# Maximum rows of the softmax: transposed alone and placed by transfers, in an attention kernel on one Trainium2 core

## The chip, the cores and the metric

The kernel runs on one core of a Trainium2 chip. The engines of the core work side by side, each in its own program's order, and meet at semaphores: PE (matrix products; its weight loads are listed as PEld), DVE (vector), ACT (activation functions and copies), POOL (general) and SP, which only issues DMA transfers here. SBUF is the memory for operands, PSUM the one that PE writes to, in banks of 128 x 512 f32. The metric is the device time of one execution in microseconds, as the median of several runs.

## The reference

Four layers act on x (4 batches, 256 rows, 160 columns) with a context (4, 512, 96). Cut to what matters:

```
def attn(x, ctx, wq, wk, wv, wo, bo, heads):       # 20 heads of 8, or 8 heads of 20
    q, k, v = heads_of(x @ wq), heads_of(ctx @ wk), heads_of(ctx @ wv)
    a = softmax(einsum('bhid,bhjd->bhij', q, k) * dh ** -0.5)
    return heads_joined(einsum('bhij,bhjd->bhid', a, v)) @ wo + bo

x = attn(x, ctx, ...) + x                          # layer 0: cross (u = 0)
for layer in (1, 3):
    x = attn(ln(x), ln(x), ...) + x                # self  (u = 1, 5)
    x = attn(ln(x), ctx, ...) + x                  # cross (u = 2, 6)
    x = (a * gelu(g)) @ ff_w2 + ff_b2 + x          # a, g = split(ln(x) @ ff_w1 + ff_b1)
    # between them layer 2: attention over 508 context rows (enc, u = 3), plus a second
    # one whose queries come from the last 4 context rows and whose keys are x (ca, u = 4)
```

The result is x after layer 3. Everything is f32 outside; softmax subtracts each row's maximum.

## The kernel before

An attention is cut into quads of four heads; there are 116 of them: 60 in cross attention, 40 in self attention, 8 in enc and 8 in ca. Queries and keys are transposed and stacked so that a head takes 32 partitions (20-head attentions, four heads in a group of 128) or 64 (8-head ones, two heads in a group). A head's partitions hold a high and a low part of each value, and two rows for its maximum: in the query stack (`qs20`, `qs8`) two columns for each head, at 3 dh and 3 dh + 1, hold the negated row maximum, as a high and a low part, and the keys hold ones there. The product of the transposed queries `qT` and the keys then already is score minus maximum, and ACT applies the exponential straight to it.

The steps of a quad are:

- `kdma`: SP copies the quad's four key heads from `kdense` to one of four places in `ring` (four transfers)
- `max` (L794 on PE, L1221 on DVE): scores in natural layout into one of two PSUM banks, and their maximum over the keys. Eight units in a cross quad, four in a self quad; `qT` still has zeros in its maximum rows here
- `negm` (L1234, L1235 on DVE): the negated maximum, and its rest, into the query stack
- `mtr` (L808 on PE, L1244 on DVE): the quad's part of the query stack is transposed again, now with the maxima, and copied over `qT`
- `st` (L775 on PE, L1062 on ACT), the slots: transposed scores of two heads and 128 keys, and the exponential. Eight in a cross quad, four in a self quad
- `pv` (L831 on PE) and `oev` (L1069 on ACT): outputs, four heads and 128 keys at a time, and their copy

Before a quad's first attention of a batch, `m_zero` (L1384, POOL) sets the stack's maximum columns to zero, so that the first transposition of the queries (`q_tr`, L938) leaves zeros.

The order of all this is one list, made by `plan()` before the program is written. Each step has a due place among the slots (`put`), a cost and a list of what it needs; `simulate` takes, again and again, the step that can start first on a modelled PE clock. Projections, layer norms, feed-forward and the transposition of queries and keys are background steps, spread among the quads of the other batch of a pair. Each engine then walks through the same list and runs its part of each step. `M_LEAD = 8` puts a quad's `mtr` eight slots before its first one. A step of kind SPARE, `mtr` among them, takes one of three PSUM banks (`sp_ps`) in turn; `taken` is the wait until the bank's reader is done with that step.

## Time and profile before

| | |
|---|---|
| median of 3 runs | 1082.69 us (1079.75 to 1086.96) |
| the profiled execution | 1083.78 us, its span 1082.0 us |
| PE / DVE / ACT / POOL busy | 96% / 64% / 62% / 7% |
| granted PE clock, mean | 0.981 |

The span is the time from the first instruction to the last; what lies around it makes the 1.8 us to the execution's time. A busy engine is not one at its peak: matmuls overlap, and each is shown with its whole latency. Idle time before an instruction is listed with what ended it. A clock of 1.00 stands for 2.4 GHz, one of 0.50 for 1.2 GHz.

### The profile page before, as it was taken

The numbers are of one execution on the slowest core, as the hardware profiler recorded it, in microseconds if no ns is written. First come the engines' busy times: TensorE is split into PE (matmuls) and PEld (weight loads), VectorE is DVE, ScalarE is ACT, GpSimd is POOL, SyncE is SP. The second block draws the span as 40 slices with busy tenths as digits, with TensorE's granted clock in tenths as the row PEclk, the third lists the DMA queues.
The fourth block names the chain that finished last, engine by engine and source line by source line (L and its number), as shares of the span: only waits on it lengthen the run. The fifth ranks groups of instructions, "written<-read, shape, count | busy, mean of one in ns | idle before, by whom it ended". The sixth has DMA issues, their size and how long they took to land.

```text
span 1082.0 us, 21250 instructions
## 1 busy us (share of the span) xinstructions
PE 1034.7 (96%) x7808; PEld 719.5 (67%) x7808; DVE 689.4 (64%) x1603; ACT 675.4 (62%) x1400; POOL 74.0 (7%) x129
## 2 busy tenths in 40 slices
PE   8999989999998999999998998999999899999978
PEld 5656666667685666767685666676768566765646
DVE  3777757875546567875755775787555556777631
ACT  4556666766664666766765665776665556766641
POOL 3000000000002100001010000000100110000000
PEclk9899999999999999999999999999999999999995
DMA  8110001110232101010113010101021400111000
GB/s 195 42 39 17 21 22 44 30 31 11 49 77 56 25 21 45 21 31 22 35 31 89 21 26 20 45 21 31 10 60 30 103 20 22 34 25 40 11 7 7
DMA packets 31150, 40.26 MB, mean 37 GB/s; under 512 B 10324, under 2 KB 22232, under 8 KB 30728
## 3 DMA queue, kind: packets, MB, share of 16 engines
q1 hardware_dynamic: 31048, 38.89, 14.9%
q8 instruction: 65, 1.06, 0.4%
q14 instruction: 37, 0.30, 0.1%
HBM read 10.97 MB, written 0.66 MB: 11 GB/s over the span
## 4 chain that ended last, share of the span: by engine, by line
PE 87%; DVE 5%; ACT 4%; issue 3%; DMA 0%; POOLq 0%; POOL 0%; DVEq 0%; ACTq 0%
PE st_ps L775 18%; PE pv_ps L831 17%; PE mx_ps L794 17%; PE sp_ps L757 8%; PE sp_ps L758 7%; PE sp_ps L876 4%; PE sp_ps L858 3%; DVE mx L1221 2%; PE sp_ps L808 2%; PE sp_ps L950 2%; PE sp_ps L938 2%; PE sp_ps L989 2%; ACT probs L1062 2%; ACT oT L1069 1%; PE sp_ps L893 1%
## 5 line engine op out<-in xcount | busy, mean ns | idle before, releaser
L1221 DVE TENSOR_REDUCE mx<-mx_ps 128x1 f32<-128x512 f32 (+2 forms) x720 | 475.4, 685 | 184.4 <-PE mx_ps L794 181.1
L1062 ACT ACTIVATE probs<-st_ps 128x512 f32<-128x512 f32 x720 | 400.6, 597 | 184.3 <-PE st_ps L775 178.4
L794 PE MATMUL mx_ps<-ring,qT 128*128 128x512 f32 (+2 forms) x864 | 294.9, 400 | 6.9 <-issue 3.8
L775 PE MATMUL st_ps<-qT,ring 128*128 128x256 f32 (+1 forms) x1408 | 276.1, 298 | 5.4 <-ACT probs L1062 3.2
L775 PEld LDWEIGHTS st_ps<-qT,ring 128*128 128x128 f32 (+1 forms) x1408 | 217.8, 190 | 80.4 <-ACT probs L1062 40.6
L831 PE MATMUL pv_ps<-probs,v 128*9 128x256 f32 (+3 forms) x2944 | 223.8, 377 | 3.0 <-ACT probs L1062 2.3
L794 PEld LDWEIGHTS mx_ps<-ring,qT 128*128 128x128 f32 x864 | 143.5, 190 | 88.9 <-DVE mx L1221 45.7
L831 PEld LDWEIGHTS pv_ps<-probs,v 128*9 128x9 f32 (+2 forms) x2944 | 44.9, 90 | 64.3 <-issue 19.2
L1111 ACT ACTIVATE kdense<-sp_ps 128x512 f32<-128x512 f32 (+2 forms) x116 | 57.4, 539 | 24.4 <-PE sp_ps L876 23.9
L1049 ACT ACTIVATE ks<-sp_ps 128x320 fp32r<-128x320 f32 x80 | 35.2, 440 | 42.3 <-PE sp_ps L858 27.5
L876 PE MATMUL sp_ps<-identr,ks 128*128 128x128 f32 (+1 forms) x416 | 59.7, 279 | 0.7 <-DVE qs L1187 0.6
L1351 POOL TENSOR_SCALAR rstd<-mv 128x2 f32<-128x2 f32 x24 | 5.6, 234 | 788.8 <-DVE mv L1258 788.8
L876 PEld LDWEIGHTS sp_ps<-identr,ks 128*128 128x128 f32 (+1 forms) x416 | 55.4, 195 | 3.5 <-DVE ks L1187 0.9
L1069 ACT ACTIVATE oT<-pv_ps 128x256 f32<-128x256 f32 x108 | 41.6, 385 | 24.8 <-PE pv_ps L831 24.2
L1244 DVE CAST qT<-sp_ps 128x256 fp32r<-128x256 f32 (+1 forms) x108 | 47.0, 435 | 14.3 <-PE sp_ps L808 13.2
L757 PE MATMUL sp_ps<-hT,wb 80*128 80x256 f32 x160 | 53.2, 417 | 1.4 <-ACT hT L1121 1.2
L758 PE MATMUL sp_ps<-hT,wb 80*128 80x256 f32 x160 | 52.3, 411 | 0.0
L1304 DVE SCALAR_TENSOR_TENSOR gate<-sp_ps,cols,gate 128x256 f32<-128x256 f32 x40 | 16.8, 478 | 54.1 <-ACT gate L1167 33.6
L808 PEld LDWEIGHTS sp_ps<-identr,qs 128*128 128x128 f32 (+1 forms) x248 | 38.7, 189 | 16.1 <-issue 13.6
L808 PE MATMUL sp_ps<-identr,qs 128*128 128x128 f32 (+1 forms) x248 | 48.3, 282 | 0.3 <-DVE ks L1187 0.3
L1187 DVE TENSOR_TENSOR ks<-sp_ps,ks 128x160 fp32r<-128x160 f32 x80 | 25.1, 317 | 36.4 <-ACT v L1090 21.5
L1293 DVE TENSOR_TENSOR x<-sp_ps,xb 128x320 f32<-128x320 f32 x32 | 15.7, 492 | 39.0 <-PE sp_ps L989 20.8
(134 smaller groups left out, 1050.2 us busy)
## 6 DMA issues: line engine op xcount, KB each, us to landing
ring<-kdense SPq DMA_DIRECT2D x256, 64.0 KB, 2.0
wb<-in_w_blk SPq DMA_DIRECT2D x4, 1400.0 KB, 9.1
ring<-kdense SPq DMA_DIRECT2D x160, 32.0 KB, 1.8
ring<-kdense SPq DMA_DIRECT2D x32, 127.0 KB, 2.3
wd<-in_w_down SPq DMA_DIRECT2D x4, 400.0 KB, 9.5
ring<-oT SPq DMA_DIRECT2D x16, 64.0 KB, 3.2
ctx_n<-in_ctx SPq DMA_DIRECT2D x4, 192.0 KB, 6.6
x<-in_x SPq DMA_DIRECT2D x4, 160.0 KB, 3.3
```

The lines of the kernel that those rows point to most:

```text
L757: pe.matmul(out, lhs[:, 0, :], rhs[:, 0, :], start=True, stop=False)
L758: return pe.matmul(out, lhs[:, 1, :], rhs[:, 1, :], start=False, stop=True)
L775: mm = pe.matmul(st_ps[s % N_ST][0:kr, i * a["nq"]:(i + 1) * a["nq"]], key_op(n, h)[:, c * P:c * P + kr], query_op(u, b)[:, h // of(u), :] ...
L794: mm = pe.matmul(mx_ps[o % N_MX][0:rows, j * a["nk"]:(j + 1) * a["nk"]], query_op(u, b)[:, h // of(u), tt * P:tt * P + rows], key_op(n, h) ...
L808: mm = pe.matmul(bank[:, k * a["nq"] + i * P:k * a["nq"] + i * P + rows], query_stack(u, b)[0:rows, t, g * of(u):(g + 1) * of(u), :].rearr ...
L831: mm = pe.matmul(pv_ps[32 * j:32 * j + a["dh"] + 1, 0:a["nq"]], v, probs[0:kr, s % N_P, i * a["nq"]:(i + 1) * a["nq"]], start=(c == 0), st ...
L876: mm = pe.matmul(bank[:, k * SQ + t * P:k * SQ + t * P + kr], ks[0:kr, t, g * of(u):(g + 1) * of(u), :].rearrange("p h s -> p (h s)"), ide ...
L1062: nc.scalar.activation(probs[0:kr, s % N_P, 0:w], st_ps[s % N_ST][0:kr, 0:w], ACT.Exp, scale=float(a["dh"]) ** -0.5).then_inc(S["probs_rea ...
L1069: nc.scalar.activation(dst, pv_ps[:, 0:ATT[u]["nq"]], ACT.Copy).then_inc(S["out_taken"], 1)
L1111: nc.scalar.activation(dst, bank[:, 0:n * SQ].rearrange("p (g k) -> p g k", g=n)[:, :, 0:w], ACT.Copy).then_inc(free, 1)
L1221: nc.vector.tensor_reduce(mx[b][0:rows, t, heads[0]:heads[-1] + 1], mx_ps[(o - 1) % N_MX][0:rows, 0:a["hpm"] * a["nk"]].rearrange("p (h k) ...
L1244: nc.vector.tensor_copy(query_op(u, b)[:, g0:g1, :].rearrange("p g q -> p (g q)"), bank[:, 0:(g1 - g0) * nq]).then_inc(done, 1)
```

## The change

The second transposition of the query stack goes. The negated maxima of a quad (8 values for each of two tiles of 128 queries) are written to a small tile of their own, `mn`; one matmul transposes it (72 columns wide, so that both tiles' rows come out, at partitions 0 and 64), DVE copies the result to `mT`, and SP puts its rows into the maximum rows of `qT` by transfers of two rows of 128 queries, a high and a low one: eight for a quad of 32-row heads (four heads, two tiles), four in enc, two in ca. That is the new step `mdma`. The first slot of a quad waits for those transfers (`m_in`) and no longer for DVE's copy. `mn` and `mT` exist twice, and DVE waits with the copy for the transfers of two quads before. As the stack's maximum columns are never written now, `m_zero` goes. The planner gives `mtr` a lower cost and `mdma` 400 ns and the latency of a transfer, 2000 ns.

```diff
-        put(hi + MTR_DUE, 3, ("mtr", n))
+        put(hi, 3, ("mtr", n))
+        put(hi, 4, ("mdma", n))
...
+    if kind == "mdma":
+        return 0, [("dma", 400)]
...
-        return TR * groups * len(q_tiles(u)), dve(groups * nq)
+        return TR, dve(P)
...
-            return [("mtr", slots[s]["n"])] + ...
+            return [("mdma", slots[s]["n"])] + ...
...
-        done[step] = t + (DMA_LATENCY if step[0] == "kdma" else HANDOFF)
+        done[step] = t + (DMA_LATENCY if step[0] in ("kdma", "mdma") else HANDOFF)
...
+        mn = [sb(f"mn{i}", [P, TQ, 64], FR) for i in range(2)]
+        mT = [sb(f"mT{i}", [72, P], FR) for i in range(2)]
...
+                    elif step[0] == "mdma":
+                        n = step[1]
+                        u, b, qd = quads[n]["u"], quads[n]["b"], quads[n]["qd"]
+                        k, sr, dh = of(u), ATT[u]["sr"], ATT[u]["dh"]
+
+                        taken(sp, ("mtr", n))
+                        for i, (t, rows) in enumerate(q_tiles(u)):
+                            for j in range(k):
+                                src = mT[n % 2][64 * i + j:64 * i + 8:k, 0:rows].bitcast(F32)
+                                at = slice(sr * j + 3 * dh, sr * j + 3 * dh + 2)
+                                g0, g1 = 4 * qd // k, 4 * (qd + 1) // k
+                                sp.dma_start(query_op(u, b)[at, g0:g1, i * P:i * P + rows].bitcast(F32), src).then_inc(m_in[n % 2], 16)
...
                         if s == quads[n]["start"]:
-                            taken(pe, ("mtr", n))
+                            pe.wait_ge(m_in[n % 2], m_landed[n])
...
-                        for k, g in enumerate(gs):
-                            for i, (t, rows) in enumerate(q_tiles(u)):
-                                mm = pe.matmul(bank[:, k * a["nq"] + i * P:k * a["nq"] + i * P + rows],
-                                               query_stack(u, b)[0:rows, t, g * of(u):(g + 1) * of(u), :].rearrange("p h s -> p (h s)"),
-                                               identr[0:rows, 0:rows], start=True, stop=True)
-                        mm.then_inc(full, 1)
+                        rows = q_tiles(u)[0][1]
+                        pe.matmul(bank[0:72, 0:rows], mn[n % 2][0:rows, :, :].rearrange("p t m -> p (t m)")[:, 0:72],
+                                  identr[0:rows, 0:rows], start=True, stop=True).then_inc(full, 1)
...
-                        link(nc.vector.tensor_scalar(st[:, :, :, 3 * dh], m, -1.0, None, ALU.mult))
...
+                        link(nc.vector.tensor_scalar(out[:, :, 0:4], m, -1.0, None, ALU.mult))
...
-                        nc.vector.tensor_copy(query_op(u, b)[:, g0:g1, :].rearrange("p g q -> p (g q)"),
-                                              bank[:, 0:(g1 - g0) * nq]).then_inc(done, 1)
+                        if n >= 2:
+                            dve.wait_ge(m_in[n % 2], m_landed[n - 2])
+                        rows = q_tiles(u)[0][1]
+                        nc.vector.tensor_copy(mT[n % 2][0:72, 0:rows], bank[0:72, 0:rows]).then_inc(done, 1)
...
-                        nc.gpsimd.memset(query_stack(u, b)[:, tiles[0][0]:tiles[-1][0] + 1, :, 3 * dh:3 * dh + 2].bitcast(F32), 0.0).then_inc(S["m_zeroed"], 1)
```

The plan's new costs move steps. Lines have moved too: in the changed kernel the slots are L800, the maxima L819, the outputs L852, the transposition of the maxima L831. Here is PE's program at the second quad's transposition, in the first cross attention, before:

```order
L794 MATMUL mx_ps0<-ring,qT0 128x512 [waits max_taken,ring_in1,spare_taken2]
L794 MATMUL mx_ps1<-ring,qT0 128x512 [waits max_taken]
L808 MATMUL sp_ps2<-identr,qs200 128x128 [waits negm_ready,spare_taken2]
L808 MATMUL sp_ps2<-identr,qs200 128x128
L794 MATMUL mx_ps0<-ring,qT0 128x512 [waits max_taken]
L794 MATMUL mx_ps1<-ring,qT0 128x512 [waits max_taken]
L775 MATMUL st_ps0<-qT0,ring 128x256 [waits spare_taken2]
L775 MATMUL st_ps0<-qT0,ring 128x256
L775 MATMUL st_ps1<-qT0,ring 128x256 x2
```

and now:

```order
L819 MATMUL mx_ps0<-ring,qT0 128x512 [waits max_taken,ring_in1,spare_taken2]
L819 MATMUL mx_ps1<-ring,qT0 128x512 [waits max_taken]
L831 MATMUL sp_ps2<-identr,mn0 72x128 [waits negm_ready,spare_taken2]
L819 MATMUL mx_ps0<-ring,qT0 128x512 [waits max_taken]
L819 MATMUL mx_ps1<-ring,qT0 128x512 [waits max_taken]
L819 MATMUL mx_ps0<-ring,qT0 128x512 [waits max_taken]
L819 MATMUL mx_ps1<-ring,qT0 128x512 [waits max_taken]
L819 MATMUL mx_ps0<-ring,qT0 128x512 [waits max_taken]
L819 MATMUL mx_ps1<-ring,qT0 128x512 [waits max_taken]
L800 MATMUL st_ps0<-qT0,ring 128x256 [waits max_rows_in0]
```

All six maximum units that the next quad has left stand between the transposition and the first scores now, where there were two; the scores wait for the transfers (`max_rows_in0`) and not for DVE's copy (`spare_taken2`). In the first self attention (quad 12), PE's program from the transposition to the quad's first scores is now:

```order
L831 MATMUL sp_ps0<-identr,mn0 72x128 [waits negm_ready,spare_taken0]
L800 MATMUL st_ps0<-qT0,ring 128x256 [waits probs_ready]
L800 MATMUL st_ps0<-qT0,ring 128x256
L800 MATMUL st_ps1<-qT0,ring 128x256 [waits probs_ready]
L800 MATMUL st_ps1<-qT0,ring 128x256
L852 MATMUL pv_ps<-probs,v200 9x256 [waits probs_ready,out_taken]
L852 MATMUL pv_ps<-probs,v200 9x256 x3
L819 MATMUL mx_ps0<-ring,qT0 128x256 [waits max_taken,ring_in1,spare_taken2]
L819 MATMUL mx_ps0<-ring,qT0 128x256
...
L800 MATMUL st_ps0<-qT0,ring 128x256 [waits probs_ready,max_rows_in0]
```

Two slots, two output groups, three maximum units and one transposition of the background stand between. On SP, the queue of all transfers, a cross quad was one group of four and is now two groups:

```order
L740 DMA ring<-kdense 32x512 [waits scores_full,spare_taken0]
L740 DMA ring<-kdense 32x512 x3
L753 DMA qT<-mT 2x128 [waits spare_taken0]
L753 DMA qT<-mT 2x128 x7
L740 DMA ring<-kdense 32x512 [waits scores_full,spare_taken0]
L740 DMA ring<-kdense 32x512 x3
L753 DMA qT<-mT 2x128 [waits spare_taken1]
L753 DMA qT<-mT 2x128 x7
```

The eight small transfers of a quad stand behind the four ring transfers of the next one, and these behind the small ones of the quad before.

## Rows read from the trace of the kernel before

**Rows 1.** Page parts 1, 2 and 4: engines; the clock by slices; the chain.
```profile
PE 1034.7 (96%) x7808; PEld 719.5 (67%) x7808; DVE 689.4 (64%) x1603; ACT 675.4 (62%) x1400; POOL 74.0 (7%) x129
...
PEclk9899999999999999999999999999999999999995
...
PE 87%; DVE 5%; ACT 4%; issue 3%; DMA 0%; POOLq 0%; POOL 0%; DVEq 0%; ACTq 0%
```

**Rows 2.** Page part 5: line, engine, tiles, count | busy us, mean ns | idle before.
```profile
L794 PE MATMUL mx_ps<-ring,qT 128*128 128x512 f32 (+2 forms) x864 | 294.9, 400 | 6.9 <-issue 3.8
L775 PE MATMUL st_ps<-qT,ring 128*128 128x256 f32 (+1 forms) x1408 | 276.1, 298 | 5.4 <-ACT probs L1062 3.2
L831 PE MATMUL pv_ps<-probs,v 128*9 128x256 f32 (+3 forms) x2944 | 223.8, 377 | 3.0 <-ACT probs L1062 2.3
L808 PE MATMUL sp_ps<-identr,qs 128*128 128x128 f32 (+1 forms) x248 | 48.3, 282 | 0.3 <-DVE ks L1187 0.3
```

**Rows 3.** Timelines of PE, PEld and DVE: start, length, line, tiles, count.
```profile
405.23 1.34 PE L876 MATMUL sp_ps<-identr,ks 128*128 128x128 f32 x10
...
46.45 0.44 PE L808 MATMUL sp_ps<-identr,qs 128*128 128x128 f32 x2
46.82 0.62 PE L831 MATMUL pv_ps<-probs,v 128*9 128x256 f32 x8
47.37 0.74 PE L794 MATMUL mx_ps<-ring,qT 128*128 128x512 f32 x2
...
53.86 0.44 PE L808 MATMUL sp_ps<-identr,qs 128*128 128x128 f32 x2
54.39 0.42 DVE L1244 CAST qT<-sp_ps 128x256 fp32r<-128x256 f32 x1
55.12 0.19 PEld L775 LDWEIGHTS st_ps<-qT,ring 128*128 128x128 f32 x1
```

**Rows 4.** DVE's groups by form; then a handoff in the timeline.
```profile
L1244 DVE CAST qT<-sp_ps 128x256 fp32r<-128x256 f32 x100 | 41.5, 415 | 7.9 <-PE sp_ps L808 7.0
L1244 DVE CAST qT<-sp_ps 128x512 fp32r<-128x512 f32 x8 | 5.5, 692 | 6.4 <-PE sp_ps L808 6.2
L1235 DVE SCALAR_TENSOR_TENSOR qs<-mx,qs 128x8 fp32r<-128x8 f32 x108 | 18.9, 175 | 3.7
...
403.20 0.41 DVE L1244 CAST qT<-sp_ps 128x256 fp32r<-128x256 f32 x1
403.66 0.54 PEld L775 LDWEIGHTS st_ps<-qT,ring 128*128 128x128 f32 x4 [0.61 <-DVE qT L1244]
```

**Rows 5.** SP's queue: L727's durations (min/median/max), then timelines.
```profile
L727 SPq DMA_DIRECT2D ring<-kdense x448: 461/591/2031, 23.8 to 1007.6; - x150
L727 SPq DMA_DIRECT2D ring<-oT x16: 467/597/602, 264.2 to 842.3; - x16
...
52.99 2.41 SPq L727 DMA_DIRECT2D ring<-kdense  x4
13.46 0.70 SPq L703 DMA_DIRECT2D ca_n<-in_ctx  x2
```

**Rows 6.** Page part 6: transfers, count, KB each, median us to landing.
```profile
ring<-kdense SPq DMA_DIRECT2D x256, 64.0 KB, 2.0
wb<-in_w_blk SPq DMA_DIRECT2D x4, 1400.0 KB, 9.1
ring<-kdense SPq DMA_DIRECT2D x160, 32.0 KB, 1.8
```

**Rows 7.** Stretches: us, busy and count by engine, PEclk; and a timeline.
```profile
12.00:23.80 11.80, 9.54 (x62) 7.69 (x61) 1.79 (x5) 9.09 (x24) 1.53 (x4) 1.00 0.94 229
23.80:34.10 10.30, 10.30 (x33) 8.38 (x33) 2.49 (x6) 5.13 (x14) 0.00 (x0) 0.50 0.52 119
40.00:77.00 37.00, 36.49 (x289) 21.16 (x289) 29.50 (x57) 23.25 (x44) 0.00 (x0) 1.00 0.13 31
...
27.57 2.48 PE L876 MATMUL sp_ps<-identr,ks 128*128 128x128 f32 x10
```

More of the change, by code:

```diff
@@ L350, in needs @@
         if kind == "negm":
-            return [("max", step[1], len(quads[step[1]]["items"]) - 1)]
+            return [("max", step[1], len(quads[step[1]]["items"]) - 1)] + ([("mtr", step[1] - 2)] if step[1] >= 2 else [])
         if kind == "mtr":
-            return [("negm", step[1])]
+            return [("negm", step[1])] + ([("mdma", step[1] - 2)] if step[1] >= 2 else [])
+        if kind == "mdma":
+            return [("mtr", step[1])]
         if kind == "st":
             s = step[1]
-            return [("mtr", slots[s]["n"])] + ([("st", s - N_ST)] if s >= N_ST else []) + ([pv_of[s - N_P]] if s >= N_P else [])
+            return [("mdma", slots[s]["n"])] + ([("st", s - N_ST)] if s >= N_ST else []) + ([pv_of[s - N_P]] if s >= N_P else [])
         if kind == "pv":
@@ L574, in build @@
         spare_taken = [sem(f"spare_taken{i}") for i in range(N_SP)]
+        m_in = [sem(f"max_rows_in{i}") for i in range(2)]
         ring_in = [sem(f"ring_in{i}") for i in range(RING)]
@@ L602, in build @@
         ring_dmas = {n: 4 * (n // RING + 1) for n in range(len(quads))}
+        m_landed, n_dma = {}, [0, 0]
+        for q in quads:
+            n_dma[q["n"] % 2] += of(q["u"]) * len(q_tiles(q["u"]))
+            m_landed[q["n"]] = 16 * n_dma[q["n"] % 2]
         used_after, count = {}, 0
@@ L1373, in _ @@
                                                 bias[:, c:c + D].unsqueeze(1).broadcast_to([P, TQ, D]), ALU.add).then_inc(S["x_biased"], 1)
-                    elif kind == "m_zero":
-                        _, u, b = step
-                        first = [q["n"] for q in quads if q["u"] == u and q["b"] == b][0]
-                        before = [q["n"] for q in quads[:first] if q["b"] % 2 == b % 2 and
-                                  (q["u"] == u if u in (3, 4) else ATT[q["u"]]["sr"] == 32)]
-                        if before:
-                            taken(pool, ("mtr", before[-1]))
-                        tiles = q_tiles(u)
-                        dh = ATT[u]["dh"]
-                        nc.gpsimd.memset(query_stack(u, b)[:, tiles[0][0]:tiles[-1][0] + 1, :, 3 * dh:3 * dh + 2].bitcast(F32), 0.0).then_inc(S["m_zeroed"], 1)
 def kernel(**inputs):
```

37 lines of the change are left out of this document (15 added, 22 removed).

## The prediction

> **What bounds the kernel now.** First the page's busy shares and its chain [rows 1]: PE is busy for 96% of the span and carries 87% of the chain, its clock is at 8 or more tenths in every slice but the last. So a saved microsecond of PE can be a saved microsecond of span, and one in which PE waits is a lost one. Then the groups [rows 2]: the scores (L775), the maxima (L794) and the outputs (L831) lead; the transposition that is changed (L808) is 248 matmuls. Their mean durations are latencies that overlap. What a matmul costs is the distance between starts [rows 3]: ten transposing matmuls in 1.34 us make (1.34 - 0.28)/9 = 0.118; a scores slot (two matmuls) or a maximum unit takes about 0.24, a group of eight output matmuls 0.55 (46.82 to 47.37). So priced the program is 845 us of PE: 720 slots 173, 720 maximum units 173, 368 output groups 195, some 1,430 transposes 164, projections and feed-forward 140. The span is 1,082, so the units of PE's program pass at 1.28 us of span for each us of price; the rest is waiting for ACT, for DVE and for signals, mostly in pieces of half a microsecond.
>
> Last, the step itself in that timeline [rows 3]. L808 starts at 53.86, L1244's copy runs 54.39 to 54.81, and 0.31 later PE loads the weights of the next block's scores (55.12), with two maximum units before it. A block of four heads (I call it a quad) lasts 7.41 us here (46.45 to 53.86), and its maximum rows are in place 0.95 us after the transposition starts. That path is short, and it is the one that the change lengthens.
>
> **What is removed.** 248 matmuls become 116, one for each quad: 132 x 0.118 = 15.6 us of PE. I take 13 as gained, as some of it lies where PE will wait anyway. DVE's copy is of 128 columns in place of 256 or 512: 415 ns and 692 ns [rows 4] give 1.08 ns a column and a constant of 138, so an estimated 277 ns; 116 copies save 17 us of DVE, which is not the bound. The DVE operations of a quad's negated maxima (175 ns for the second [rows 4]) stay as they are. The 28 memsets of POOL run beside all else, as POOL is busy 7%: nothing; if they held up a transposition at all, it could only be a gain.
>
> **What is added.** Eight transfers for each quad of 32-row heads (100 quads), four in the enc attention and two in the ca attention (8 each): 848, all issued by SP, after the copy and one after the other. SP does not issue for free [rows 5]: a ring transfer holds its queue for 591 ns (median of 448), and four of them take 2.41 us from first start to last end, so the distance is (2.41 - 0.59)/3 = 0.61. The least rows with few descriptors are two loads of four rows each, 0.70 us together, 0.35 each. These read DRAM and stand at the start; the ring rows go from SBUF to SBUF in mid-kernel, as the new ones do, but with 32 rows. Ends: 0.35 and 0.61. I take 0.55, nearer the ring rows because those of 64 rows (from oT, 597) cost the same as those of 32 (from kdense, 591), so it isn't the number of rows that makes them dear. Landing: 1.8 us for 32 KB and 2.0 for 64 KB [rows 6]; the size matters little, so 1.8 for 1 KB.
>
> The Trainium skill, "DMA: Bandwidth & Descriptors", section on the anatomy of one DMA, puts the fixed cost at about 2.0 us, nearly all of it completion, whatever the size. By that the estimate below would be 0.2 us longer for each quad that waits, some 17 us in all, 1,210 in place of 1,193; the ring rows here agree to within that.
>
> The new path from the matmul to the scores of its quad is then: matmul 0.28 and 0.09 until the copy (54.30 to 54.39), copy 0.28, signal to SP 0.05, seven distances of 0.55, landing 1.80, signal to PE 0.05: 2.55 + 7 x 0.55 = **6.4 us**, where it was 0.95. The 0.05 is from a copy that PE waits for, 403.61 to 403.66 [rows 4]. With 0.35 the path is 5.0, with 0.61 it is 6.8. For four transfers it is 4.2, for two 3.1.
>
> **What hides it.** PE is in order, so only what the program has put between the two counts. The planner allows a transfer step 0.4 us of issue and 2.0 of latency, about 3.3 from matmul to scores, and moves the work so: in the order of the change six maximum units and two output groups lie there in one cross quad, four slots, four maximum units and three output groups in the next. I counted what stands between the two for all 116 quads, priced it as above and multiplied by 1.28:
> - cross attention, 60 quads: mean 6.2 us, but 39 of them are under 6.4, with a mean of 4.9: 39 x 1.5 = 58 us of new waiting
> - self attention, 40 quads: 38 are under 6.4, with a mean of 3.8: 38 x 2.57 = 98 us. Its quads have four slots and not eight, so there is less to put in between
> - enc attention, 8 quads: 6 under 4.2, mean 3.3: 5 us. ca attention: none
>
> Sum 161 us. Part is given back: while PE waits, ACT and DVE empty their buffers, so what follows, up to the next transposition, meets fewer waits. That is 223 us of priced PE work behind the quads that wait; passing at 1.1 in place of 1.28, my guess between 1.28 and the 1.0 of a PE that never waits, it gives back 40.
>
> What is queued behind: SP runs 12 issues a quad now, 4 x 0.61 + 8 x 0.55 = 6.8 us. That is under the 10.3 us that a quad would take on average (1,193/116), so the queue isn't the bound; self attention has the shorter quads, and there the waiting counted above stretches them beyond it. SP's old wait before each group, for the scores of four quads before, is older than all it now stands behind. Four times the block's weights go out on the same queue and take 9 us to land [rows 6]; a quad's transfers behind them could be late by a few microseconds, 4 x 5 = 20 at most, which the range holds. DVE's new wait for the transfers of two quads before is met long before. PE's wait stands at a quad's first scores, and everything behind it on PE waits along; ACT and DVE follow within two buffers.
>
> **The sum.** 1,083.8 (the profiled execution; its span is 1,082.0 and the median of the three runs 1,082.7, so it stands for them) + 161 - 40 - 13 = 1,192: I say **1,193**.
>
> **The rivals.**
> - *The clock falls as well.* PE's clock was at 0.50, which is 1.2 of 2.4 GHz, from 23.8 to 34.1 us; before that came 11.8 us in which PE was busy for 9.54 (81%) [rows 7]. From 40 to 77 it is busy for 36.49 of 37 and the clock is full. With a wait of 2 us in each quad of 10, PE would be busy for about 80%, like the stretch before the fall. At half clock, matmuls cost double (ten in 2.48 us, not 1.34 [rows 7]), so a stretch of 10.3 us loses up to 5 us, less what hides in the waits; one such stretch in every 60 us, at 3.5 us each, is 20 x 3.5 = 70: 1,263. Against it: the waits are short and spread. The Trainium skill, "TensorE: Matmul & The Clock Gate", section on HAM oscillation, describes this case: a loop in which every wait for a DMA lowers the clock again. By that rule the time would be this rival's.
> - *Small transfers are issued at the cheapest distance seen, 0.35.* The path is 5.0 us; the same count gives 64 of waiting, 31 back, 13 gained: 1,083.8 + 20 = 1,104. For it: nothing in the trace shows an SBUF transfer of two rows. Against it: the two sizes of ring transfers cost the same.
> - *The path is hidden and PE's saving remains.* Faster: 1,083.8 - 15.6 = 1,068. It decides where the path is under the planner's own 3.3 us, which is what the order is laid out for, i.e. (3.3 - 2.55)/7 = 0.11 us an issue. The least issue in the rows is 0.35 [rows 5].
>
> **Numbers.** Forecast 0.52; clock 0.22; cheap issues 0.19; hidden 0.04; 0.03 between the last two, within a per cent. Three rounds of this kernel scatter by 0.7%, so 1% is about what can be told. The range takes in 0.42 an issue with the give-back (94 - 35 - 13, 1,130), 0.61 without it (196 - 13, 1,267) and most of the clock's case, which adds to either: 1,125 to 1,300. It leaves out half of the cheapest issues and the hidden case. Faster 0.04, same 0.03, slower 0.93.
>
> **What would show it.** The distance between the new transfers' issues on SP, and their landing; some 6.4 us from the new matmul to the first scores of its quad in place of 0.95 at the least; PE's waits before L800 (the scores) put down to the transfer into qT, more than half of the total in self attention, though it is a third of the quads; PEclk below 9 in slices where the clock's rival holds. I am wrong in the first place if an issue takes under 0.3 us, in the second if PE's waits for DVE and ACT shrink by more than 40 us.

## The result and the profile after

The changed kernel takes **1471.1 us** (median of 4 runs, 1456.0 to 1485.4) against 1083.8 for the kernel before (4 runs, 1079.8 to 1087.0): ratio 1.353, 95% interval 1.341 to 1.365. The forecast was 1,193 with a range of 1,125 to 1,300. The side was right, the size was not: the loss is 387 us where 110 was forecast. The profiled execution is the longest of the four, 1485.4 us with a span of 1483.6; it ran at a lower clock than the other three and is left out of the ratio. The sums below are made against its own span and the 1082.0 of before.

The page, parts 1, 2 and 4, in the order of [rows 1]: engines with busy time, share and instructions; the granted clock in 40 slices; the chain by engine.

```profile
PE 1221.2 (82%) x7676; PEld 820.5 (55%) x7676; DVE 679.5 (46%) x1603; ACT 690.3 (47%) x1400; POOL 71.2 (5%) x103
...
PEclk9788877789876876897998988889989667779896
...
PE 50%; SPq 25%; DMA 10%; DVE 6%; issue 6%; ACT 2%; POOLq 0%; POOL 0%; DVEq 0%; ACTq 0%
```

PE is 132 instructions shorter and 187 us longer busy. Its idle time, span less busy time, was 47 us and is 262. The chain, 87% PE before, now runs for a third through SP's queue and the transfers. The clock read 9 in 38 of 40 slices before; it reads 9 in 11 now, and 6 to 8 in the other 29.

The groups that answer to [rows 2] and the waits behind them (line, what was waited for: us in total, times, longest):

```profile
L800 PE MATMUL st_ps<-qT,ring 128*128 128x256 f32 (+1 forms) x1408 | 336.0, 348 | 189.5 <-DMA qT<-mT 180.4
...
L819 PE MATMUL mx_ps<-ring,qT 128*128 128x512 f32 (+2 forms) x864 | 333.3, 449 | 31.1 <-issue 23.2
L852 PE MATMUL pv_ps<-probs,v 128*9 128x256 f32 (+3 forms) x2944 | 256.8, 430 | 2.9 <-ACT probs L1080 1.4
```

```profile
PE st_ps L800 <- DMA qT<-mT: 180.4, 87, 9.1
...
PEld mx_ps L819 <- issue: 85.6, 139, 7.6
...
PEld st_ps L800 <- ACT probs L1080: 57.1, 114, 0.8
...
PEld mx_ps L819 <- DVE mx L1239: 48.9, 99, 1.0
```

The first row of the waits is the change: 180 us at the first scores of 87 quads, where the forecast had 161 us in 83. Two more things are to be seen in the groups. The same 1,408 score matmuls have a mean of 348 ns in place of 298, the maxima 449 in place of 400, the outputs 430 in place of 377. And the weight loads' waits for ACT's and DVE's buffers, 57.1 and 48.9, did not shrink; before they were:

```profile
PEld mx_ps L794 <- DVE mx L1221: 45.7, 113, 0.7
...
PEld st_ps L775 <- ACT probs L1062: 40.6, 98, 0.7
```

The step itself, in the timelines of PE, DVE and SP (start, length; the wait before it in brackets):

```profile
57.38 0.22 PE L831 MATMUL sp_ps<-identr,mn 128*72 128x128 f32 x1
...
60.65 1.10 PE L819 MATMUL mx_ps<-ring,qT 128*128 128x512 f32 x2 [0.18 <-DVE mx L1239]
64.28 1.22 PE L800 MATMUL st_ps<-qT,ring 128*128 128x256 f32 x4 [2.53 <-DMA qT<-mT]
...
66.85 0.31 PE L831 MATMUL sp_ps<-identr,mn 128*72 128x128 f32 x1
...
73.88 0.50 PE L800 MATMUL st_ps<-qT,ring 128*128 128x256 f32 x2 [1.63 <-DMA qT<-mT]
```

```profile
58.08 0.28 DVE L1261 CAST mT<-sp_ps 72x128 fp32r<-72x128 f32 x1
```

```profile
58.39 4.86 SPq L753 DMA_DIRECT2D qT<-mT  x8
63.36 2.43 SPq L740 DMA_DIRECT2D ring<-kdense  x4
67.51 5.27 SPq L753 DMA_DIRECT2D qT<-mT  x8
72.90 2.43 SPq L740 DMA_DIRECT2D ring<-kdense  x4
```

```profile
L753 SPq DMA_DIRECT2D qT<-mT x832: 562/563/682, 36.7 to 1438.8; - x167
```

Matmul at 57.38, copy 58.08 to 58.36, eight issues from 58.39 to 63.25, scores at 64.28: a path of 6.90, and 7.03 for the next quad (the median of the 83 quads of 32-row heads that wait is 6.91). An issue holds the queue 0.563 us, and eight in 4.86 us make a distance of (4.86 - 0.563)/7 = 0.614. The last issue starts at 62.69 and its rows are in 1.59 us later. The row on SP also shows how tight its queue is here: small ones, keys, small ones, keys, with the keys of the next quads issued only when the small ones are out.

Last, the clock. Stretches of the same timeline (length; busy time and count on PE, PEld, DVE, ACT, POOL; PEclk; DMA share; GB/s):

```profile
48.80:62.50 13.70, 11.92 (x91) 6.04 (x83) 9.88 (x18) 6.49 (x13) 0.00 (x0) 1.00 0.09 22
62.50:69.30 6.80, 4.76 (x21) 3.31 (x22) 0.63 (x3) 2.58 (x5) 0.00 (x0) 0.50 0.16 39
69.30:86.40 17.10, 12.54 (x94) 6.41 (x93) 11.36 (x21) 6.97 (x14) 0.00 (x0) 1.00 0.07 18
```

At 62.5, inside the wait of 2.53 us, the clock goes to 0.50, 1.2 GHz, and is back at 2.4 GHz at 69.3. In the kernel before, the stretch from 40 to 77 was at full clock without a break [rows 7]. The clock stands at 1.00 or at 0.50, so the mean over the span, 0.832, makes 2 x (1 - 0.832) x 1483.6 = 498 us at half clock; before, 0.981 makes 41. The 498 us lie in 61 stretches. What that costs is what the experiments have to show: it can be the slower matmuls, or something else can lengthen the busy time.

### The profile page after: what moved, and what is told of

The parts are those of the page before. It is cut to its first block, busy times and chain, and to the rows that moved or that the text cites. A ratio compares the mean times of both kernels' runs of the same rounds, so it can differ in the third digit from the quotient of the medians.

```text
span 1483.6 us, 21914 instructions
## 1 busy us (share of the span) xinstructions
PE 1221.2 (82%) x7676; PEld 820.5 (55%) x7676; DVE 679.5 (46%) x1603; ACT 690.3 (47%) x1400; POOL 71.2 (5%) x103
## 4 chain that ended last, share of the span: by engine, by line
PE 50%; SPq 25%; DMA 10%; DVE 6%; issue 6%; ACT 2%; POOLq 0%; POOL 0%; DVEq 0%; ACTq 0%
SPq L753 23%; PE st_ps L800 13%; DMA qT<-mT 9%; PE mx_ps L819 8%; PE pv_ps L852 7%; PE sp_ps L782 6%; PE sp_ps L783 5%; DVE mx L1239 3%; PE sp_ps L897 3%; PE sp_ps L956 2%; PE sp_ps L879 2%; PE sp_ps L1007 1%; DVE mT L1261 1%; SPq L740 1%; PE sp_ps L968 1%
## 5 line engine op out<-in xcount | busy, mean ns | idle before, releaser
L800 PE MATMUL st_ps<-qT,ring 128*128 128x256 f32 (+1 forms) x1408 | 336.0, 348 | 189.5 <-DMA qT<-mT 180.4
L800 PEld LDWEIGHTS st_ps<-qT,ring 128*128 128x128 f32 (+1 forms) x1408 | 260.1, 228 | 295.5 <-DMA qT<-mT 209.8
L819 PE MATMUL mx_ps<-ring,qT 128*128 128x512 f32 (+2 forms) x864 | 333.3, 449 | 31.1 <-issue 23.2
L852 PE MATMUL pv_ps<-probs,v 128*9 128x256 f32 (+3 forms) x2944 | 256.8, 430 | 2.9 <-ACT probs L1080 1.4
L819 PEld LDWEIGHTS mx_ps<-ring,qT 128*128 128x128 f32 x864 | 167.8, 223 | 136.6 <-issue 82.3
L1261 DVE CAST mT<-sp_ps 72x128 fp32r<-72x128 f32 (+1 forms) x116 | 32.3, 279 | 141.4 <-PE sp_ps L831 141.4
L852 PEld LDWEIGHTS pv_ps<-probs,v 128*9 128x9 f32 (+2 forms) x2944 | 47.0, 92 | 80.0 <-issue 39.8
L897 PE MATMUL sp_ps<-identr,ks 128*128 128x128 f32 (+1 forms) x416 | 70.0, 307 | 1.8 <-DVE ks L1205 1.0
L897 PEld LDWEIGHTS sp_ps<-identr,ks 128*128 128x128 f32 (+1 forms) x416 | 65.7, 224 | 8.2 <-issue 5.2
L968 PE MATMUL sp_ps<-ident,oT 128*128 128x128 f32 x216 | 34.5, 297 | 14.1 <-ACT oT L1087 13.8
L782 PE MATMUL sp_ps<-wb,hT 80*128 80x160 f32 (+1 forms) x128 | 44.1, 431 | 1.2 <-ACT hT L1147 0.8
```

The lines of the kernel that those rows point to most:

```text
L782: pe.matmul(out, lhs[:, 0, :], rhs[:, 0, :], start=True, stop=False)
L800: mm = pe.matmul(st_ps[s % N_ST][0:kr, i * a["nq"]:(i + 1) * a["nq"]], key_op(n, h)[:, c * P:c * P + kr], query_op(u, b)[:, h // of(u), :] ...
L819: mm = pe.matmul(mx_ps[o % N_MX][0:rows, j * a["nk"]:(j + 1) * a["nk"]], query_op(u, b)[:, h // of(u), tt * P:tt * P + rows], key_op(n, h) ...
L852: mm = pe.matmul(pv_ps[32 * j:32 * j + a["dh"] + 1, 0:a["nq"]], v, probs[0:kr, s % N_P, i * a["nq"]:(i + 1) * a["nq"]], start=(c == 0), st ...
L897: mm = pe.matmul(bank[:, k * SQ + t * P:k * SQ + t * P + kr], ks[0:kr, t, g * of(u):(g + 1) * of(u), :].rearrange("p h s -> p (h s)"), ide ...
L968: mm = pe.transpose(bank[0:rows, k * P:(k + 1) * P], src, ident[:, :])
```

## The experiments

The theory after the result: the loss is idle time of PE (215 us more) and, caused by it, half clock (457 us more), which makes the busy time 187 us longer. The rivals: the new order of the steps is what costs; SP's queue holds the keys back, whoever waits; the transfers disturb by their number; the planner's wrong prices are the cause.

**A. The new order with the old data flow** (`e5_order`): the kernel before, its planner changed as in the diff, its transposition and copy untouched.

```diff
+        put(hi, 4, ("mdma", n))
-        return TR * groups * len(q_tiles(u)), dve(groups * nq)
+        return TR, dve(P)
-        done[step] = t + (DMA_LATENCY if step[0] == "kdma" else HANDOFF)
+        done[step] = t + (DMA_LATENCY if step[0] in ("kdma", "mdma") else HANDOFF)
```

> The kernel before, data flow and all (second transposition of the query stack, no small transfers), with its steps in the order that the changed planner makes, but for some ties. With no transfer on any path this is the price of the new order alone. Theory O2 (the order, which keeps the scores back 3.3 us behind the transposition, costs what is left in the kernel with two transfers, 1,181 us): 1,150 to 1,185. If what is left there is the two transfers' own path: 1,075 to 1,110.

Measured: 1142.2 us (1140.8 to 1146.4), ratio 1.054 (1.049 to 1.059): just below the 1,150 to 1,185 of the theory that the order costs, and far from the 1,075 to 1,110 of the other. The order alone is 58 us; 2,210 of PE's 2,448 steps stand in the places that they have in the changed kernel. By itself it is a small part of 387, and in F it proves a help to the changed kernel, not a harm.

**B. The transfers without PE's wait for them** (`e1_nowait`), to tell the queue from the wait. They go to rows of a tile that nobody reads, and PE waits for DVE's copy alone. What this kernel leaves out is the subtraction of the maxima, so its results are not those of the attention; ACT's scale is made smaller to keep the exponentials finite.

```diff
-                            pe.wait_ge(m_in[n % 2], m_landed[n])
+                            taken(pe, ("mtr", n))
...
-                                sp.dma_start(query_op(u, b)[at, g0:g1, i * P:i * P + rows].bitcast(F32), src).then_inc(m_in[n % 2], 16)
+                                r = 32 + 16 * (n % 2) + 8 * i + 2 * j
+                                dst = cpT[r:r + 2, 0:(g1 - g0) * rows].rearrange("p (g q) -> p g q", g=g1 - g0)
+                                sp.dma_start(dst, src).then_inc(m_in[n % 2], 16)
```

> All 848 transfers are issued as in the changed kernel, but into rows that nothing reads, and PE's first scores of a quad wait for DVE's copy alone. So the maxima are not subtracted from the scores; the exponential gets a twentieth of its scale to stay finite. Theory W (PE's wait for the transfers, and the half clock that follows from PE's idle time, make all of the 387 us): about 1,085, between 1,065 and 1,110, with a granted clock over 0.97. Theory O (the new order of the steps costs the time): over 1,250, as the order is the same. Theory Q (848 more issues on SP crowd its queue and delay the keys): over 1,250, as they are all still there.

Measured: 1363.1 us (1345.7 to 1365.2), ratio 1.255 (1.246 to 1.264). The theory that PE's wait makes all of the loss, about 1,085, fails. PE waits for no small transfer and the kernel is still 221 us slower than the order alone. PE's waits and SP's timeline in this kernel:

```profile
PEld mx_ps L823 <- issue: 184.0, 141, 7.8
PE mx_ps L823 <- issue: 131.4, 59, 7.3
```

```profile
68.67 5.27 SPq L755 DMA_DIRECT2D cpT<-mT  x8
74.06 2.43 SPq L740 DMA_DIRECT2D ring<-kdense  x4
81.30 4.86 SPq L755 DMA_DIRECT2D cpT<-mT  x8
86.26 2.43 SPq L740 DMA_DIRECT2D ring<-kdense  x4
```

The wait has moved to the maxima, and it is put down to "issue", since no record names a releaser; the first maximum of a quad starts with the landing of its keys. In SP's rows the keys start where the small transfers end, and these start only when DVE's copy of their quad is done: the keys issued at 86.26 could have gone at 76.5, when SP was free, but stand behind the transfers of another quad, whose copy is ready at 81.3. That this is the wait is shown by moving them:

**The same with the keys ahead** (`e6_keys`): SP issues the keys of the next quads before it waits for a quad's copy, where the ring has room (100 of 116 quads). And **the keys ahead, with PE's wait** (`e7_keys_wait`), the changed kernel otherwise.

```diff
+                    if step[0] == "mdma" and step[1] + 2 < len(quads):
...
+                            for m in (q["n"] - 1, q["n"]):
+                                if m not in early and place["kdma", m] > place[step]:
+                                    early.add(m)
+                                    sp_order.append(("kdma", m))
```

> The kernel whose transfers nobody on PE waits for (1,363 us), with one thing changed: SP issues the keys of the quad after next ahead of a quad's small transfers, and so ahead of their wait for DVE's copy, for 100 of 116 quads. Small transfers, PE's program and order are the same. Theory Q (SP is in order, so the ring transfers stand behind the small ones, and PE waits for keys: 132 us of waits for landed ring transfers in that trace): those waits go, 1,160 to 1,200, as in the kernel with two transfers. If crowding of the DMA engines themselves mattered: over 1,300.

> The changed kernel with the same move of the keys on SP, PE's wait for the small transfers in place. Theory Q as a cause beside the path: in the trace of the changed kernel PE waits 22 us for landed keys and 180 for small transfers, so at most some 30 us come off 1,471: 1,440 to 1,471. If the two waits hide each other and the path alone sets the time: no change within 1%. If late keys also made the transposition late, and so the path: under 1,400.

Measured: 1163.4 us (1154.4 to 1177.9), ratio 1.071 (1.064 to 1.078), without the wait; 1459.2 (1455.1 to 1466.3), 1.347 (1.341 to 1.354), with it. Both are where their expectations put the theory of the keys. PE's longest wait, first without and then with its wait for the rows:

```profile
PE mx_ps L837 <- issue: 16.8, 11, 2.7
```

```profile
PE st_ps L814 <- DMA qT<-mT: 190.0, 89, 8.9
```

So 848 transfers that are issued and land cost 21 us over the order alone (that kernel has 132 matmuls more, some 13 us, so perhaps 34): their number disturbs little. The keys behind them cost 200 us, but only where PE does not wait for the rows anyway; once it does, they hide behind that wait (12 us are left, which the two intervals do not tell from none). And the wait for the rows costs 296 us, the half clock that comes with it included.

**C. A shorter path.** Two transfers a quad (`e4_two`): two matmuls transpose the tiles side by side into 8 rows, and one transfer carries the high rows of all four heads, one the low ones. The order is that of the changed kernel.

```diff
-                        for i, (t, rows) in enumerate(q_tiles(u)):
-                            for j in range(k):
-                                src = mT[n % 2][64 * i + j:64 * i + 8:k, 0:rows].bitcast(F32)
-                                at = slice(sr * j + 3 * dh, sr * j + 3 * dh + 2)
+                        for j in range(2):
+                            if k == 4:
+                                src = mT[n % 2][4 * j:4 * j + 4, 0:nq].bitcast(F32)
+                                at = slice(3 * dh + j, 3 * dh + j + 3 * sr + 1, sr)
```

> Two transfers for each quad in place of eight: both tiles of queries are transposed into the same eight rows (two small matmuls), and one transfer carries the high rows of four heads, one the low rows, each into four rows of qT that lie 32 apart. Order and planner as in the changed kernel. The path is 0.37 + 0.28 + 0.03 + 1 x 0.61 + 1.6 + 0.11 = 3.0 us, below what the planner allows. Theory W: hardly any wait, full clock: 1,070 to 1,110. Theory O: over 1,250. If the landing and not the issues was what mattered, the waits fall by half only: about 1,270.

Measured: 1180.6 us (1176.4 to 1187.9), ratio 1.091 (1.085 to 1.096), between the 1,070 to 1,110 of the theory of the wait and the 1,250 and more of the order: 58 of the 97 us that are left are the order's (A). PE's wait for the rows is now:

```profile
PE st_ps L807 <- DMA qT<-mT: 20.6, 9, 8.7
```

Six distances of 0.6 us less on the path are worth 290 us. With `M_LEAD = 12` in place of 8, the transposition four slots earlier (`e8_lead`):

> Two transfers for each quad, as in the kernel of 1,181 us, and M_LEAD = 12 in place of 8: a quad's maxima and their transposition are due four slots earlier, so the path of 3.0 us lies beside scores of the quad before and not in front of its own. If the order is what costs 97 us there: 1,075 to 1,130. If it is the path or the queue: 1,150 or more.

Measured: 1162.7 us (1158.9 to 1175.4), ratio 1.075 (1.068 to 1.082): 18 us less. The expectation had 1,075 to 1,130 if this lead could take away what the order costs; it cannot, and most of the 97 us stay.

**Two queues** (`e12_two_queues`): the eight transfers again, but those of the second tile are issued by POOL, so that four stand behind one another and not eight.

```diff
+                        if len(q_tiles(u)) == 2:
+                            taken(pool, ("mtr", n))
+                            for j in range(k):
+                                src = mT[n % 2][64 + j:72:k, 0:P].bitcast(F32)
...
+                                nc.gpsimd.dma_start(query_op(u, b)[at, g0:g1, P:2 * P].bitcast(F32), src).then_inc(g_in[n % 2], 16)
```

> The changed kernel with the four transfers of the second query tile issued by POOL, the first four by SP, same order, same number of transfers. It tells the number of transfers from their standing in one queue. If the path is issue distance times number in the queue, and POOL issues as fast as SP (0.56), the path is 4 x 0.56 = 2.2 us shorter, 4.7, and SP holds the keys back 2.2 us less: the waits fall from 180 to about 60, and the time to 1,230 to 1,300 (on the line between eight transfers, 1,471, and two, 1,181, a path of 4.7 gives 1,310). If the transfers themselves or their semaphore are what takes the time, it stays near 1,471. If POOL issues at over 1 us each, the path is not shorter and the time is near 1,471 or above, while SP's distance is unchanged: the page then shows POOL's issues as the last to land.

Measured: 1253.1 us (1236.9 to 1256.3), ratio 1.153 (1.144 to 1.161). Its durations of issues, and its waits:

```profile
L1390 POOL DMA_DIRECT2D qT<-mT x416: 518/518/737, 37.5 to 1205.0; - x139
```

```profile
PE st_ps L804 <- DMA qT<-mT: 41.3, 30, 8.7
...
PE st_ps L804 <- issue: 21.8, 12, 4.0
```

POOL issues about as fast as SP. The 12 waits put down to "issue" stand at first scores too, so the wait of 180 us is now 63, near the 60 expected, and 218 us of time are gone with the same number of transfers and bytes. The Trainium skill, "DMA: Bandwidth & Descriptors", section "Issuing engines are not separate DMA queues", says that starting transfers from several engines saves only the time to initiate them, which is usually small beside the transfer. For one transfer that holds here, 0.56 us beside a landing of 1.6; but eight wait for one another, and seven distances are 4.3 us of a path of 6.9.

**D. The clock alone** (`e2_fill`): the changed kernel, with matmuls of nothing (128 columns, result overwritten) in front of PE's wait in 84 of the 87 quads that wait, as many as fill the wait at 0.118 us each, 1,480 in all. PE still waits for the same rows; it is only not idle.

```diff
+                            for _ in range(FILL.get(n, 0)):
+                                pe.matmul(st_ps[s % N_ST][:, 0:P], identr[:, :], identr[:, :], start=True, stop=True)
                             pe.wait_ge(m_in[n % 2], m_landed[n])
```

> The changed kernel with filler matmuls (128 columns, into the scores bank that is overwritten next) ahead of PE's wait in the 84 quads that waited, as many as fit in the wait that the trace shows. The waits stay, the clock should not fall. Theory W with the clock as the larger part: the clock is over 0.95 and the time is what the waits alone cost, 1,083.8 + 180 - 40 - 13 = 1,211, between 1,180 and 1,260. If the half clock costs little, since it falls while PE would wait anyway: over 1,400.

Measured: 1409.5 us (1401.8 to 1412.7), ratio 1.300 (1.294 to 1.306): more work on PE, and 62 us less time. The expectation had 1,180 to 1,260 if the clock was the larger part of the loss, and over 1,400 if half clock costs little because it falls where PE would wait anyway; the time is in the second. Page part 1 and the groups that count:

```profile
PE 1279.6 (91%) x9156; PEld 918.9 (65%) x9156; DVE 677.6 (48%) x1603; ACT 683.7 (49%) x1400; POOL 71.4 (5%) x103
```

```profile
L824 PE MATMUL mx_ps<-ring,qT 128*128 128x512 f32 (+2 forms) x864 | 312.3, 423 | 27.3 <-issue 19.0 <-DVE mx L1244 5.9 <-ACT kdense L1134 0.4
L805 PE MATMUL st_ps<-qT,ring 128*128 128x256 f32 (+1 forms) x1408 | 304.7, 319 | 54.7 <-DMA qT<-mT 40.8 <-ACT probs L1085 12.6
L857 PE MATMUL pv_ps<-probs,v 128*9 128x256 f32 (+3 forms) x2944 | 234.5, 394 | 5.6 <-ACT probs L1085 3.7 <-ACT oT L1092 1.3
L798 PE MATMUL st_ps<-identr 128*128 128x128 f32 x1480 | 183.0, 279 | 0.0
```

Mean clock 0.930, so 197 us at half clock and not 498. All the kernel's own matmuls are busy for 1279.6 - 183.0 = 1096.6 us, where they were for 1221.2: 125 us less for 301 us less at half clock, 0.41 for one. (14.6 us of the filler lie beneath the kernel's own matmuls; counted with these they are 110 us less, 0.37 for one.) The mean latencies go back from 348, 449 and 430 ns to 319, 423 and 394.

Why is the kernel then only 62 us faster, 77 by the spans? What PE stands still or fills has grown, from 262 us to 127 + 183 = 310. The path did not get shorter with the higher clock: over the waiting quads of 32-row heads its median is 6.91 us in both kernels. Here is the quad that waited for 2.53 us above, its transposition at 62.91:

```profile
67.12 2.46 PE L798 MATMUL st_ps<-identr 128*128 128x128 f32 x21
69.82 0.74 PE L805 MATMUL st_ps<-qT,ring 128*128 128x256 f32 x4 [0.25 <-DMA qT<-mT]
```

The path is again 6.91 us. Where the work that hides it gets faster, more of the path is left to wait for, so part of what the clock costs lies in time that PE would wait anyway; this fits the growth and is not shown quad by quad. (Some of the 48 us are filler that ran on after the rows were in, by my estimate about 23 us in ten quads, with 1.59 us of landing taken for each.)

**E. The planner told the truth.** The changed kernel with 4,850 ns of issue and 1,600 of landing for `mdma` in place of 400 and 2,000 (`e3_planner`), and the one with two transfers with 1,200 and 1,600 (`e11_two_planner`).

```diff
-        return 0, [("dma", 400)]
+        return 0, [("dma", 4850)]
```

> Only the planner's figures are changed: 4,850 ns of issue for a quad's transfers in place of 400, and 1,600 of latency, as the trace shows them (eight at 606 ns, landing 1.60 us after the last issue). By the same count as in the prediction, with the measured path of 6.8 us, the work put between the transposition and the scores grows from 6.2 to 8.6 us in cross and from 4.0 to 5.7 in self attention, and the waiting falls from 194 to 70 us. Theory W: waiting and half clock fall alike, 1,083.8 + 387 x 70/194 = 1,223, between 1,160 and 1,290. Theory O: no better than 1,450, since the order moves further away from the old one.

> The kernel with two transfers a quad, and the planner told their measured price: 1.2 us of issue and 1.6 of landing in place of 0.4 and 2.0. The planner's sum from matmul to scores grows by 0.4 us, so only the few quads with a wait left (20 us in all) gain. Theory: the waits go to about 10 us and the order's price stays at 50 to 60: 1,165 to 1,180 against 1,181. Rival: as with eight transfers, the planner moves other waits in, for DVE and ACT, and nothing is gained: 1,180 to 1,200. Faster than before's 1,084 by neither.

Measured: 1418.9 us (1413.3 to 1421.5), ratio 1.308 (1.302 to 1.315), and 1172.1 (1166.7 to 1177.3), 1.083 (1.078 to 1.087). The first is far above the 1,160 to 1,290 that were expected if waiting and half clock fell alike; the second is as expected, and its interval meets that of the kernel without the true prices. For eight transfers the waits for them nearly go, and others come:

```profile
PEld mx_ps L819 <- DVE mx L1239: 100.4, 204, 1.1
...
PEld st_ps L800 <- ACT probs L1080: 85.0, 173, 1.0
...
PE sp_ps L831 <- DVE mn L1252: 38.0, 36, 1.6
...
PE st_ps L800 <- DMA qT<-mT: 27.0, 12, 4.3
```

against 48.9, 57.1, 0.8 and 180.4. PE is idle 192 us (1419.7 - 1227.9) where it was 262, yet at half clock for 454 us (clock 0.840), nearly as long. So the wrong prices are worth 52 us of the 387. The right ones make the order cover a path of 6.5 us, and PE waits elsewhere instead: for the negated maxima at the transposition (38 us), and its weight loads for DVE's and ACT's buffers. That the covering work is what these places lack is argued, not shown.

**F. The old order with the new data flow**: the planner's old prices, so that 2,098 of PE's 2,448 steps stand in the place that they had before, with eight transfers (`e9_old8`) and with two (`e10_old2`).

```diff
-        return TR, dve(P)
+        return TR * (4 * a["sr"] // P) * len(q_tiles(u)), dve(4 * a["sr"] // P * nq)
-        return 0, [("dma", 400)]
+        return 0, []
```

> The changed kernel's eight transfers a quad in the list that the planner of before would make (the planner's costs of mtr and st as before, mdma free), so nearly the order of before. It tells what the changed order is worth. By the account of waits: the priced work between the matmul and the scores, times 1.28, is 2.0 to 4.2 us a quad there, against a path of 6.9: about 430 us of waits, 1,084 - 13 + 430 = 1,500, and more with the clock's part (the changed kernel's clock was 0.84): 1,500 to 1,620. If instead the changed order is itself what costs (the two-transfer kernel and the kernel with the order alone were both slower than before), this one comes out at or under the changed kernel's 1,471.

> Two transfers a quad (path about 3.1 us) in nearly the order of before. By the account of waits: 97 us of waiting, less 13 for the matmuls saved, no price for the order: 1,168, between 1,150 and 1,190, near the two-transfer kernel in the changed order (1,181), which pays 58 for the order and little for waits. If the order's 58 us is a real price and the short waits are given back by relief of ACT and DVE, it is well below: 1,110 to 1,140. If waits of under a microsecond in nearly every quad lower the clock, it is above 1,200.

Measured: 1780.4 us (1773.6 to 1792.7), ratio 1.646 (1.638 to 1.653), and 1323.9 (1315.4 to 1339.2), 1.222 (1.213 to 1.231). The first is far above what was expected, the second where its expectation put the clock's case. The new order costs 58 us by itself and saves 309 with eight transfers, 143 with two: it is what keeps the loss at 387. Page part 1 of the first:

```profile
PE 1332.9 (74%) x7676; PEld 896.5 (50%) x7676; DVE 681.3 (38%) x1603; ACT 694.7 (39%) x1400; POOL 71.5 (4%) x103
...
PEclk9788766888976666787878876678885676668886
```

```profile
PE st_ps L800 <- DMA qT<-mT: 371.5, 98, 8.5
```

The waits are 372 us, under the 430 counted. The loss is 709 us between the spans. What the expectation put too low is the clock again, for which it left up to 120 us: it is at 0.750, so 895 us at half clock, and PE is busy for 298 us more.

## Why the prediction failed

One table carries it. Idle is span less PE's busy time, both from page part 1; half clock is 2 x (1 - mean clock) x span. For the filled kernel the busy time is without the filler's 183, which are not in its idle time either.

| kernel | span | PE busy | idle | half clock |
|---|---|---|---|---|
| before | 1082.0 | 1034.7 | 47 | 41 |
| new order alone | 1144.7 | 1067.1 | 78 | 89 |
| two transfers, true prices | 1164.9 | 1068.2 | 97 | 105 |
| two transfers, lead 12 | 1173.7 | 1082.9 | 91 | 148 |
| two transfers | 1174.6 | 1075.5 | 99 | 136 |
| no wait for the rows, keys ahead | 1176.1 | 1085.6 | 90 | 167 |
| two queues | 1252.2 | 1107.2 | 145 | 218 |
| two transfers, old order | 1315.7 | 1133.5 | 182 | 300 |
| no wait for the rows | 1363.4 | 1156.7 | 207 | 344 |
| changed, filled | 1406.9 | 1096.6 | 127 | 197 |
| changed, true prices | 1419.7 | 1227.9 | 192 | 454 |
| changed, keys ahead | 1464.5 | 1215.3 | 249 | 483 |
| changed | 1483.6 | 1221.2 | 262 | 498 |
| changed, old order | 1790.9 | 1332.9 | 458 | 895 |

Two ratios hold over the table, measured from the first row. For each us more at half clock PE is busy 0.35 to 0.53 us longer where the half clock is over 100 us (the changed kernel: 186.5/457 = 0.41); the filler, which takes the half clock away and gets the busy time back, shows that this is cause and effect. And for each us more of idle time there are 1.8 to 2.2 us more at half clock in the kernels that idle over 120 us, but 2.9 in the one with the true prices, which I cannot explain; under 120 us it is anything from 1.3 to 2.9. Together a microsecond more of idle time comes with about 1 + 0.4 x 2 = **1.8 us** more of span. For the changed kernel: 215 x 1.8 = 387 of the 402 us between the spans. For the old order with eight transfers: 411 x 1.8 = 740, measured 709. This is bookkeeping and no test, as span is idle plus busy time and the two ratios come from the same rows. Nor is the 0.8 what a kept clock would give back: the filler took away two thirds of the added half clock, 301 of 457 us, and the span fell by 77 of the 402.

By the prediction's own steps:

- *The path*: right within half a microsecond. 6.4 us was forecast, 6.9 and 7.0 measured. The distance was 0.61 and not 0.55: it is that of the ring rows [rows 5], the upper end; an issue of 2 rows holds the queue for 0.563 us, one of 32 rows for 0.591. From the matmul's start to the copy's it was 0.70 and not 0.37. The landing was 1.6 and not 1.8, which took part of that back; the copy was 0.28 as estimated. The 2.0 us that the prediction gives from the Trainium skill, "DMA: Bandwidth & Descriptors", section on the anatomy of one DMA, are stated there for transfers issued by GpSimd; here those of SP are in after 1.6 us, and those that POOL issues (`e12_two_queues`) after 1.5, the median of 416.
- *What hides it*: right in sum, 180 us in 87 quads for 161 in 83, with errors by kind that cancel in part, which is luck: 82 us in cross attention (58 forecast), 78 in self attention (98, so it is under half of the total and not over), 20 in enc (5). Of these 20, 18 are two waits, 9.1 and 9.0 us, that the prediction named and left to the range: the small transfers behind the block's weights on the queue, here on SP and on PE:

```profile
423.18 0.35 SPq L711 DMA_DIRECT2D wb<-in_w_blk  x1
423.57 0.43 SPq L713 DMA_DIRECT2D wd<-in_w_down  x1
424.05 0.43 SPq L713 DMA_DIRECT2D wbc<-in_w_blkc  x1
424.52 2.68 SPq L753 DMA_DIRECT2D qT<-mT  x4
```

```profile
433.99 1.23 PE L800 MATMUL st_ps<-qT,ring 128*128 128x256 f32 x4 [9.11 <-DMA qT<-mT]
```

- *The saving of 13 us on matmuls*: nothing speaks against it, and nothing could show it beside 387.
- *The clock, which the sum leaves out*: **the step that failed most**. The sum has no term for it, so PE should have been busy 13 us less; it was busy 187 us longer. That is 200 of the 294 us between the sum's 1,192 and the profiled 1485.4. The reason for leaving it out, "the waits are short and spread", was wrong: with waits of 2.1 us in the mean, in 87 quads, PE was at half clock for 457 us more.
- *The give-back of 40 us*: **the second step that failed**. It read the factor of 1.28 between priced work and span as waiting that a pause of PE could relieve. There was less of that than it needs: PE idled for 47 us in all before the change, and its weight loads' waits for DVE and ACT went up with it, from 86.3 to 106.0 us. The pause gave nothing back that the runs show. The sign named for this, that these waits shrink by more than 40 us, pointed the wrong way.
- *SP's queue is not the bound*: wrong in its argument, of little weight in the result. I looked at what the small transfers stand behind, not at what stands behind them: the keys of the next quad wait for a copy that they do not need. Alone that costs 200 us (B); beside the wait for the rows 12.
- *The order*: not priced at all. It costs 58 us by itself.
- *The clock's rival*: the mechanism that made the forecast miss its range, given 0.22. It is not the larger part of the loss: of the 402 us between the spans 215 are idle time, and of the other 187 some would have been waiting at full clock (D). Its price for a stretch, 3.5 us for 10.3 at half clock, is 0.34 for one and near the 0.41 measured. Its number was wrong: 20 stretches, 206 us, where 457 came. I had taken the one stretch of the trace before [rows 7] for the measure of how rarely such a wait lowers the clock. The trace after shows a fall inside a wait of 2.53 us, after 13.7 us in which PE was busy for 11.9. The Trainium skill, "TensorE: Matmul & The Clock Gate", section on HAM oscillation, describes waits for transfers that lower the clock again in every turn of a loop. The trace agrees that such waits lower it again and again, with PEclk below 9 in 29 of 40 slices, but not that each one does: there are 61 stretches at half clock for 87 waits. The filler agrees too.

With the waits as counted and the factor of 1.8, which only these runs give, the sum would have been 1,084 + 161 x 1.8 - 13 = 1,361; the rest is 54 us more of idle time than counted (19 at the first scores, 19 at the maxima, where "issue" went from 3.8 to 23.2, the remainder in small waits), 97 with its part of the clock: 1,458.

What stays open: why the true prices leave the half clock at 454 us with so much less idle time, which of the order's moves cost its 58 us and what the changed kernel would take at full clock throughout. No version tried beats the kernel before. The nearest with the change, two transfers and the longer lead, is 7.5% slower; the 13 us that the change can save are less than what two transfers and their order cost.

## What to carry to other kernels

Where PE is the bound and its clock is full, price a new wait of PE at nearly twice its length, as it came out here, and not at less: the pause lowers the clock of the work behind it. Do not count on getting that back by filling the wait: of the loss of 387 us that gave back 62. Small transfers (1 KB here) cost their place in the issuing queue, 0.6 us each; put as many rows into one as a pattern can hold, or split them over two queues, before anything else, and look at what stands behind them as well as ahead. If a step's path grows, ask first whether the order can cover it: here the order was worth 309 us, and still lost.

## What the runs showed of the hardware

- An issue of a transfer between places of SBUF takes SP nearly the same time whatever its size: 0.563 us for 1 KB in two rows, 0.591 for 64 KB in 32, 0.671 for the 1.5 KB of the ca attention; at 0.61 between starts (after, L753; before, L727). POOL takes 0.518 for the small one (two queues, L1390).
- Rows of 1 KB are in 1.6 us after the last issue starts, as seen by PE.
- PE's clock fell to half 0.75 us into a wait of 2.53 us, after 13.7 us at full clock in which PE was busy for 11.9; in the kernels that idle for over 120 us, 1.8 to 2.9 us at half clock come with each us more of idle time.
- A microsecond at half clock cost 0.41 us of busy time in the changed kernel, and 0.37 to 0.41 by the filler, less than the 0.5 by which matmuls at double cost [rows 7] would fall short.
- Matmuls of nothing in place of waiting made a kernel 62 us faster (1471.1 to 1409.5), with 1,480 more of them, while PE's idle time and the filler together grew by 48 us and the path to the rows kept its median of 6.91 us.
